# Causal attention and an fp4 net in one block with written orders, the rounding's comparisons added up on TensorE

## The reference

```python
# causal attention, two sequences of 1024 tokens, one head of 128
Q, K, V = (einsum(x, W) + b for each)
scores = where(tril, einsum('bqh,bkh->bqk', Q, K), -inf)
attn = softmax(scores * 128 ** -0.5, axis=-1)
out = einsum(attn, V) @ Wo.T + bo

# fp4 net, hidden width 352
def fp4_quant_dequant(x):                    # blocks of 16 along the last dim
    scale = maximum(max(abs(xb)) / 6.0, 1e-12)
    idx = searchsorted([0.25, 0.75, 1.25, 1.75, 2.5, 3.5, 5.0], abs(xb / scale))
    return [0, 0.5, 1, 1.5, 2, 3, 4, 6][idx] * sign(xb) * scale
fp4_linear = lambda x, w: einsum('bsk,nk->bsn', fp4_quant_dequant(x), fp4_quant_dequant(w))
h = silu(fp4_linear(x, w_gate)) * fp4_linear(x, w_up)
return fp4_linear(h, w_down)
```

## Time and profile before

| | us |
|---|---|
| median of three runs | 1979.06 (1977.74 to 1983.82) |
| profiled execution | 1977.1 |
| its span | 1975.4 |
| PE busy in the span | 1688.1 (85%) |
| DVE busy | 1365.1 (69%) |
| ACT busy | 1209.5 (61%) |
| POOL busy | 125.2 (6%) |
| mean granted TensorE clock | 0.928 |

### The profile page before, as it was taken

How to read it: one execution, slowest core, us unless ns; L and a number is a source line. 1 busy time by engine, 2 the same in 40 slices (tenths; PEclk the granted TensorE clock), 3 DMA queues, 4 the chain that set the end, 5 groups by cost and what they waited for, 6 DMA issues and landing times. The chain is left out here.

```text
span 1975.4 us, 19098 instructions
## 1 busy us (share of the span) xinstructions
PE 1688.1 (85%) x6799; PEld 702.5 (36%) x6799; DVE 1365.1 (69%) x1768; ACT 1209.5 (61%) x1500; POOL 125.2 (6%) x165
## 2 busy tenths in 40 slices
PE   4699999999999999968986897878989998947734
PEld 2233333333333333224432675332333343325512
DVE  4677777777777777412324785238999999947696
ACT  2488888888888888831334723137867577334411
POOL 1000111111111111210000000000000000010010
PEclk8799999999999999987997998888999999978967
DMA  3400001010101000001210000413444354300000
GB/s 114 106 6 11 22 11 27 6 27 6 27 6 33 4 14 1 1 11 71 91 45 10 1 2 7 152 46 107 154 155 166 128 180 149 101 17 1 0 0 21
DMA packets 44628, 100.71 MB, mean 51 GB/s; under 512 B 7311, under 2 KB 20718, under 8 KB 42204
## 3 DMA queue, kind: packets, MB, share of 16 engines
q1 hardware_dynamic: 44538, 99.54, 15.6%
HBM read 91.55 MB, written 7.87 MB: 50 GB/s over the span
## 5 line engine op out<-in xcount | busy, mean ns | idle before, releaser
L727 DVE TENSOR_REDUCE best<-quad 128x2 f32<-128x1024 f32 x256 | 309.7, 1221 | 130.4 <-PE quad L517 128.0
L641 ACT ACTIVATE weights<-quad 128x1024 f32<-128x1024 f32 x256 | 255.3, 1027 | 28.9 <-PE quad L542 28.6
L1206 ACT ACTIVATE e_hid<-quad,e_w1s 128x1024 f32<-128x1024 f32 x48 | 53.4, 1113 | 136.8 <-PE quad L108 136.8
L559 PE MATMUL quad<-weights,values 128*32 128x512 f32 x1024 | 136.4, 605 | 0.4 <-ACT weights L641 0.4
L2220 ACT ACTIVATE l_hid<-quad,l_w1s 128x512 f32<-128x512 f32 x112 | 74.9, 686 | 99.5 <-PE quad L108 98.8
L1222 DVE TENSOR_TENSOR e_hid<-e_hid,e_cs 128x1024 f32<-128x1024 f32 x48 | 58.0, 1224 | 111.5 <-ACT e_hid L1206 96.0
L2082 PE MATMUL quad<-l_st,ident 128*128 128x512 f32 x256 | 119.5, 594 | 6.4 <-DVE l_st L2286 6.4
L108 PE MATMUL quad<-xn,l_w1s 128*128 128x512 f32 x224 | 113.8, 621 | 10.9 <-DMA l_w2s<-in_F_w 5.3
L108 PE MATMUL quad<-q,wf 128*128 128x512 f32 x256 | 121.5, 606 | 0.7 <-DVE mk L698 0.3
L2128 PE MATMUL quad<-l_hid,l_w2s 128*128 128x512 f32 x224 | 109.5, 623 | 14.0 <-DVE l_hid L2317 14.0
L108 PE MATMUL quad<-hid,wf 128*128 128x512 f32 x256 | 116.6, 599 | 0.0
(11 more groups left out here) (383 smaller groups left out, 3010.6 us busy)
## 6 DMA issues: line engine op xcount, KB each, us to landing
e_cs<-comb SPq DMA_DIRECT2D x16, 1024.0 KB, 4.9
l_bs<-xd_dram SPq DMA_DIRECT2D x32, 512.0 KB, 4.9
l_c_rows<-xd_dram SPq DMA_DIRECT2D x32, 512.0 KB, 5.0
l_cs<-comb SPq DMA_DIRECT2D x28, 512.0 KB, 4.7
wf<-in_L_f SPq DMA_DIRECT2D x16, 256.0 KB, 2.6
l_w1s<-in_F_w SPq DMA_DIRECT2D x28, 129.0 KB, 2.1
l_w2s<-in_F_w SPq DMA_DIRECT2D x28, 128.0 KB, 2.2
q_dram<-part SPq DMA_DIRECT2D x12, 256.0 KB, 3.2
```

The costliest lines, as they stand in the source:

```text
L559: last = nc.tensor.matmul(out[32 * j:32 * j + 32, :], values[:, kt, GH * g + j, :], weights[p % BUFS][:, j % 2, j // 2, :], start=(kt == 0 ...
L641: nc.scalar.activation(weights[p % BUFS][:, slot, :, :].rearrange("p a t -> p (a t)"), doubles.of("weigh", m, i), ACT.Exp, scale=scale).th ...
L727: nc.vector.tensor_reduce(heads[:, :, slot, qt, c], doubles.of("search", m, i).rearrange("p (a t) -> p a t", a=2), AX.X, ALU.max).then_inc ...
```

## The change

Layer 3's three blocks become one, `layer_3_branches`. Attention and net are lists of generators on each engine with planned times (`PLAN_CAUSAL`, `PLAN_PIECE`, `PLAN_FP4`), and all PSUM products go through one ring of four slots. The values to round are cut into 12 pieces: gate and up weights together, x of each half, w_down, and eight of the hidden values, 704 columns each. For each piece DVE writes seven comparisons of 0 or 1 in bf16, one tensor each. PE adds them with identity matrices times 0.5, 1 and 2, accumulating in PSUM, and DVE multiplies the sum with the signed scale. Sign times scale moves from POOL to DVE. Hidden values are turned and multiplied with w_down in quarters. ACT loads the table set of exp again whenever a Silu came between. The block has its own set of semaphores, which is cleared behind it.

```diff
+W_IN, W_OUT = 2 * len(FCH) * P, FI
+MIDS = ((0.25, 0), (0.75, 0), (1.25, 0), (1.75, 0), (2.5, 1), (3.5, 1), (5.0, 2))
+STEP_OF = (0.5, 1.0, 2.0)
+PIECES = (("weights", 0, W_IN), ("x", 0, T), ("x", 1, T), ("weights", 1, W_OUT)) + tuple(("hidden", j, 2 * FI) for j in range(FT))
...
+PLAN_FP4 = {
...
+    "silu": (2001.070, 2937.502, 3430.300, 6255.737, 6296.804, 11372.474, 11422.447, 11999.578),
+    "mul": (1442.169, 2986.589, 4149.661, 10252.697, 10316.567, 11392.729, 11471.828, 11967.625),
...
+def layer_3_branches(core, a):
...
+            def _(sp):
+                for i, w_in in enumerate((a["F3_gate"], a["F3_up"])):
...
+                        sp.dma_start(raw[0:size, at:at + P], w_in[c:c + size, :]).then_inc(w_landed, 16)
+                sp.dma_start(w[:, :], a["A3_w"]).then_inc(landed, 16)
+                sp.dma_start(col[:, :], a["A3_cols"]).then_inc(landed, 16)
+                sp.dma_start(raw[:, W_IN:W_IN + W_OUT], a["F3_down"]).then_inc(w_landed, 16)
+            W_ALL = 16 * (2 * len(FCH) + 1)
...
+                def sums():
+                    for n, (kind, i, size) in enumerate(PIECES):
+                        yield piece("sum", n)
...
+                        pe.wait_ge(compared, len(FEW) * (n + 1))
+                        pe.wait_ge(compared_more, len(MANY) * (n + 1))
+                        ring_free(pe, "sum", n, 0)
...
+                            for m, (mid, step) in enumerate(MIDS):
+                                last = nc.tensor.matmul(ring.of("sum", n, 0)[:, c:end], steps[:, step, :], above[:, m, c:end],
+                                                        start=(m == 0), stop=(m == len(MIDS) - 1), skip_group_check=True)
+                        last.then_inc(summed, 1)
...
+                def exponentials(h):
...
+                        if table[0] != LN_EXP:
+                            nc.scalar.preload_act_table_set(LN_EXP)
...
+                def of_values(name, func, done):
...
+                        if kind == "weights":
+                            act.wait_ge(w_landed, W_ALL)
...
+                def signed_scales():
...
+                        nc.vector.tensor_tensor(blocks(sign), blocks(sign), over_blocks(scale), ALU.mult).then_inc(signed, 1)
...
+                def comparisons(name, mids, done):
...
+                        dve.wait_ge(in_steps, n + 1)
+                        if n >= 2:
+                            dve.wait_ge(summed, n - 1)
+                        for m in mids:
+                            nc.vector.tensor_scalar(above[:, m, :], size, MIDS[m][0], None, ALU.is_gt).then_inc(done, 1)
...
+                        nc.vector.tensor_tensor(values(n), ring.of("sum", n, 0)[:, 0:PIECES[n][2]], sign, ALU.mult).then_inc(rounded, 1)
...
-        fp4_net(core, a["F3_gate"], a["F3_up"], a["F3_down"],
-                lambda beside: causal_attention(core, a["A3_w"], a["A3_cols"], beside))
+        with core.own_semaphores():
+            layer_3_branches(core, a)
```

More of the change, by code:

```diff
@@ L2338, in _ @@
                          *(gates(h) for h in BOTH), *(join(h) for h in BOTH), choices(), weigh(), *(experts_done(h) for h in BOTH))
-def causal_attention(core, w_qkvo, cols, beside):
-    nc = core.nc
[L2347 to L2358, removed]
+FB = 16
@@ new lines, in layer_3_branches @@
+        gate = [sb(f"gate{i}", [P, 2, FI]) for i in range(2)]
+        turned_h = [sb(f"turned_h{i}", [P, len(FCH), BANK]) for i in range(2)]
+        size_t = [sb(f"size{i}", [P, T]) for i in range(2)]
+        sign_t = [sb(f"sign{i}", [P, T]) for i in range(3)]
+        over = [sb(f"over{i}", [P, len(MIDS), T], BF16) for i in range(2)]
+        stats = sb("stats", [P, 2, sum(size for kind, i, size in PIECES) // FB])
+        steps = sb("steps", [P, len(STEP_OF), P], BF16)
+        firsts = [sum(size for kind, i, size in PIECES[:n]) // FB for n in range(len(PIECES))]
@@ L2393, in _, with tokens_first @@
[L2393 to L2399, removed]
+                def tokens_first(h):
+                    yield att("xT", h)
+                    ring_free(pe, "xT", h, 0)
+                    for t in range(FT):
+                        last = nc.tensor.transpose(ring.of("xT", h, 0)[:, t * P:(t + 1) * P], half(core.xn, h)[:, t * P:(t + 1) * P], core.ident[:, :])
+                    last.then_inc(x_turned[h], 1)
@@ L2401, in scores @@
                             end = min(c + BANK, (t + 1) * P)
[L2402 to L2415, removed]
-                        for j in range(t + 1):
[L2417 to L2420, removed]
+                            nc.tensor.matmul(to[:, c:end], q[h][:, own], k[h][:, c:end], start=True, stop=(end < (t + 1) * P), skip_group_check=True)
@@ L2423, in _ @@
                                                     start=(j == 0), stop=(j == t), skip_group_check=True)
[L2424 to L2466, removed]
-                    for h in BOTH:
-                        done = core.dve_done[h]
-                        dve.wait_ge(core.act_done[h], sact.value("exp", t))
-                        nc.vector.reciprocal(st[h][:, 3:4], st[h][:, 2:3]).then_inc(done, 1)
-                        dve.wait_ge(done, sdve.value("recip", t))
-                        nc.vector.tensor_scalar(p[h][:, keys], p[h][:, keys], st[h][:, 3:4], None, ALU.mult).then_inc(done, 1)
-                    beside(dve, t)
-                dve.wait_ge(landed, 32)
-                for h in BOTH:
-                    dve.wait_ge(core.pe_done[h], spe.value("out"))
-                    nc.vector.scalar_tensor_tensor(out=half(core.x, h), in0=core.slot[h][1], scalar=col[:, 3:4], in1=half(core.x, h),
-                                                   op0=ALU.add, op1=ALU.add).then_inc(core.dve_done[h], 1)
@@ new lines, in out_of_hidden @@
+                def out_of_hidden():
+                    for r in range(QUARTERS):
+                        yield net("net", r)
+                        pe.wait_ge(out_copied, 2)
+                        pe.wait_ge(wide_copied, r + 1)
+                        pe.wait_ge(rest_copied, r + 1)
+                        product(nc, ring.of("rest", r, 0)[:, BANK:2 * BANK],
+                                [(down[0:size, n, :], turned_h[r % 2][0:size, n, :]) for n, (c, size) in enumerate(FCH)]).then_inc(net_ready, 1)
```

597 lines of the change are left out of this document (377 added, 220 removed).

## The result

The changed kernel takes 1894.34 us (median of 4 runs, 1893.32 to 1895.18) where the kernel before takes 1978.4 on the same chip; the ratio is 0.9571, with a 95% interval of 0.9551 to 0.9591. That is 84 us less. The prediction had 64 less and a range that began at 1906: the direction came, and so did both gains that it named (less work on DVE, and DVE's idle time filled); the size was 20 us short.

A forecast was written before the change was run, and what follows sets the result against it. DVE was taken to bound layer 3: 7 + 134.2 + 1.4 + 6.1 = 148.7, +11 stalls, +0.9 clearing: 160.6 instead of 224.6 us. That gave 1915, plus 1 on top: 1916 us, range 1906 to 1924 (1934 with rivals).

The forecast's parts named there:

- DVE's instructions: Layer 3: DVE's work falls to 134.2 us, 29.5 less, with comparisons at the fast price and normal-price broadcasts.
- PE's sums: Layer 3's new work on PE: 161 bf16 matmuls over 61,600 columns, 26.5 us, hidden while DVE's path is longer.
- rival B: Layer 3 on DVE: comparisons to bf16 at one column per cycle (+31) or slow broadcasts (+24): 1940 to 1947 us; chance 0.06.
- Gaps and overlaps: DVE in layer 3: 177 gaps cost 6.2 us, sixty overlapping comparisons give 4.8 back, together +1.4.
- The pair in the earlier trace: Two 256-column operations in layer 1 take 0.75 us where one takes 0.42: an overlap of 0.08 to 0.09.
- Stalls: Layer 3 between head and tail: clock losses and hops add +11 us, chosen between bounds of +3 and +18.5.
- bound of layer 1: Upper bound for layer 3's stalls: layer 1 leaves DVE idle 11.5 of 94 us (12%), which gives +18.5 us.
- Rival A: Layer 3: PE and DVE hold each other up, 12 to 22% idle: 1923 to 1943 us; chance 0.16.
- D: Layer 3: PE stays at its lower clock level, cut into short pieces, so slower than before: 2004 us; chance 0.02.
- Head and tail: Layer 3's ends: a 7 us wait for input transfers, then 7.5 us after the last rounding, 6.1 of it extra.
- rival C: Layer 3 on ACT: seven more table loads end on the path, at most 9 us: 1925; chance 0.04.
- rival E: Layer 3: the change does not interleave; DVE's 134 plus the present 61 us idle: 1951 us; chance 0.03.

## Why the prediction was right in direction and wrong in size

**DVE's instructions: right.** 134.2 us was predicted; the 237 records of layer 3 sum to 134.1. The comparisons at 0.52, the multiplication into steps at 0.88, the fast rate from f32 to bf16 and the cost of the broadcast (none) all came. PE's sums are busy for 26.1 us against 26.5. So rival B falls, and that sign times scale is about free on DVE is borne out by its return to POOL.

**Gaps and overlaps: the step that failed.** "Together +1.4" measured -11.4 (61 gaps, 2.2 us, and 165 overlaps, 13.7 us), 12.8 us off. I let 177 instructions wait for their neighbour, as in layer 3 of before, and only sixty comparisons overlap. But in the new written order only 61 instructions pay a gap for their neighbour, and 165 of 236 successions overlap: all 84 comparisons do, not sixty, and most maxima, reciprocals, block maxima and products as well, since what stands ahead of them belongs to another piece, another half or the other branch. The interleaving of attention and net is not what does it. Only 40 of the 165 overlaps lie between the branches, and with the net behind the attention 145 of them and 63 gaps remain (-10.0 us in place of -11.4). How the pieces of work are cut and sorted takes the waits off the neighbour, within each branch already. The pair in the earlier trace rows showed the overlap for a tensor_tensor, and I took it for the comparisons alone. Chaining the comparisons (+5.4 in layer 3) and chaining everything (+32.6, some 20 by the plain gap) show that these successions come out in the time. The term also had no bounds: with all 236 successions overlapping it would have been -19.6, and the range would have begun below 1890 (both are estimates).
The Trainium skill ("VectorE: DVE Perf Modes", The DRAIN you can't avoid), which the prediction weighed, says that a semaphore between operations costs nothing extra; here a wait for the neighbour costs 0.118 us, and 0.19 or more where it stands in a record of its own. The same section of the skill also says that a next operation that is not held starts earlier; the trace agrees, with 0.083 us. I had weighed the first sentence and not read the second against the new order.

**Stalls: mis-sized.** "I take +11" measured 3.6, 7.4 us off. The bound of layer 1 (12%) was far too high here, though PE and DVE are as equal as there. That the two branches cover each other's hops is shown (63.6 us of waits against 16.7 when the net stands behind), and PE's clock stayed up (0.99); why layer 1, which has a written order too, loses 12% isn't shown. Rival A falls with this, and D too: PE's granted clock was 1.00 from 1765 on. That PE had 14 us of slack was wrong as well: DVE's path became shorter than I had it, and 3 or 4 were left.

**Head and tail: right.** Head 7.6 us instead of 7, tail from the end of the last rounding to the last join 7.5 as predicted. The clearing of the semaphores was put at 0.9; between the last join and the end of the span lie 5.4 us instead of 4.5. The sum of the differences, -12.7 for gaps between head and tail, -7.4 for stalls, -0.8 for instructions (the step matrices ran inside the head), +0.6 for the head, is the 20 us.

**The tables (rival C)**: eight loads of 1.28 us were there. The 2.66 us that the Trainium skill ("ScalarE: Activation LUTs", What ACT_TABLE_LOAD costs) gives for a switch don't show here either: the ACTIVATE behind three loads starts 0.01 us after the last, and behind six of the changed kernel's eight loads it is the same (of the other two one waits for its input, and one starts 0.04 behind). The rival's price was not paid, since all of DVE's waits between head and tail are 3.6 us, but its mechanism is real, as eight more loads show.

The order without the interleaving (rival E) would have lost 48 us, as its own kernel shows, nearly all of it in waits for other engines.

What stays open: how much of the stalls' small size is due to PE's clock (0.99), since no kernel changed the clock alone, why layer 1's share of waits did not carry over, and what fewer table loads would bring, since none was run.

## What to carry to other kernels

Before an order is priced, count for each engine how many instructions wait for the one just ahead: on DVE that is 0.118 us a time here. Cutting the work into pieces and sorting them so that the next instruction needs something older took off two thirds of these gaps, within each branch already. Interleaving the two branches did another thing: it filled waits for other engines, 47 us of them. Give the count of waited neighbours a bound in the range like any other term. In an order in which two engines are both 95% busy, a third at 60% need not have room: 10 us more on ACT cost 14 us here, and 8 us moved to it, without a new plan of the order, cost 16.

## What the runs showed of the hardware that was not expected

- DVE: an instruction that waits for no neighbour starts 0.083 us before the neighbour's recorded end (163 cases in the middle of layer 3, all kinds that occur there, 158 of them 0.078 to 0.088 and the others down to 0.060), and waits that have long been met don't change this. A wait for the neighbour on the instruction itself makes it 0.035 behind the end; in a record of its own ahead of the instruction 0.10 to 0.11, with a third wait 0.13 to 0.14 (the chain of all instructions).
- A comparison from f32 to bf16 costs 0.519 us at 704 columns, as a tensor_scalar within f32 would by the price of the earlier trace rows.
- POOL beside DVE stretches DVE's comparisons too (eight beside POOL took 917 ns in the mean, 48 others 517), not only the broadcast multiplication (2534 against 1212).
- A table load of a table that is already there leaves no load in the trace, and the time didn't change (1893.09 us with four such).
- PE idle for 3.4 of 10 us in the block's head went with a granted clock of 0.66 in that window, between windows of 0.84 and 1.00.
